# Cross-attention with an FP4 feed-forward on one core: gate and up of a chunk as one alternating run of 24 matmuls

## The reference

```python
def fp4_linear(x, w):
    xq = fp4_quant_dequant(x)
    wq = fp4_quant_dequant(w)
    return jnp.einsum('bsk,nk->bsn', xq, wq)
gate = fp4_linear(x, w_gate)          # 512 -> 1408
y = fp4_linear(x, w_up)               # 512 -> 1408
h = jax.nn.silu(gate) * y
return fp4_linear(h, w_down)          # 1408 -> 512
...
x = x + _L0_ffn_ref(_layernorm(x, axis=-1), L0_ffn_w_gate, L0_ffn_w_up, L0_ffn_w_down)
```

## Time and profile before

| what | value |
|---|---|
| median of 3 runs | 1179.66 us (1179.59 to 1182.97) |
| span of the profiled execution, first to last instruction | 1176.7 us |
| TensorE busy | 1158.8 us, 98% |
| VectorE busy | 970.3 us, 82% |
| ScalarE busy | 483.5 us, 41% |
| GpSimd busy | 179.3 us, 15% |
| feed-forward, tile 2 on | from 467 us to the end |

### The profile page before, as it was taken

How to read it: one execution, slowest core, us unless ns; L and a number is a source line. 1 busy time by engine, 2 the same in 40 slices (tenths; PEclk the granted TensorE clock), 3 DMA queues, 4 the chain that set the end, 5 groups by cost and what they waited for, 6 DMA issues and landing times.

```text
span 1176.7 us, 21716 instructions
## 1 busy us (share of the span) xinstructions
PE 1158.8 (98%) x6784; PEld 1057.6 (90%) x6784; DVE 970.3 (82%) x1609; ACT 483.5 (41%) x1201; POOL 179.3 (15%) x305
## 2 busy tenths in 40 slices
PE   7899999999999999999999999999999999999998
PEld 6688888888888889999999999999999999999997
DVE  6778888888888877988888888888888888888865
ACT  3556656566566553333332332233233323333321
POOL 3433333333333310000000000000000000000000
PEclk9999999999999999999999999999999999999999
DMA  7223323323344436554445345444534454453442
GB/s 240 45 89 88 111 88 110 91 84 111 108 139 148 132 108 194 150 105 86 89 89 102 70 93 99 88 88 87 105 70 93 98 90 88 82 104 76 82 85 46
DMA packets 154955, 119.30 MB, mean 101 GB/s; under 512 B 95597, under 2 KB 122301, under 8 KB 154660
## 3 DMA queue, kind: packets, MB, share of 16 engines
q1 hardware_dynamic: 154916, 118.85, 42.7%
HBM read 74.47 MB, written 24.94 MB: 84 GB/s over the span
## 4 chain that ended last, share of the span: by engine, by line
PE 78%; SPq 7%; DMA 7%; DVE 2%; ACT 2%; issue 2%; POOL 2%; POOLq 0%; DVEq 0%; ACTq 0%
PE g_ps L175 7%; PE u_ps L175 7%; PE u_ps L176 7%; PE g_ps L176 7%; PE u_ps L177 7%; PE g_ps L177 7%; PE d_ps L1436 6%; PE d_ps L1437 6%; PE d_ps L1435 6%; SPq L504 4%; DMA ws_dram<-w_rows 4%; PE o_ps L784 3%; PE s_ps L764 3%; DMA w_wide<-ws_dram 3%; POOL w_q L586 2%
## 5 line engine op out<-in xcount | busy, mean ns | idle before, releaser
L175 PE MATMUL g_ps<-wguh,xnh 128*128 128x352 f32 x496 | 162.4, 327 | 0.5 <-issue 0.5
L175 PE MATMUL u_ps<-wguh,xnh 128*128 128x352 f32 x496 | 159.9, 322 | 0.5 <-DVE hid L1576 0.5
L176 PE MATMUL u_ps<-wgul,xnh 128*128 128x352 f32 x496 | 159.8, 322 | 0.0
L176 PE MATMUL g_ps<-wgul,xnh 128*128 128x352 f32 x496 | 159.8, 322 | 0.0
L177 PE MATMUL u_ps<-wguh,xnl 128*128 128x352 f32 x496 | 159.6, 322 | 0.0
L177 PE MATMUL g_ps<-wguh,xnl 128*128 128x352 f32 x496 | 159.5, 322 | 0.0
L898 ACT ACTIVATE probs<-s_ps,nsmax 128x77 f32<-128x77 f32 x512 | 113.7, 374 | 92.2 <-DVE nsmax L990 92.2
L1576 DVE TENSOR_TENSOR hid<-u_ps,silu 128x352 f32<-128x352 f32 x128 | 66.8, 522 | 78.1 <-PE u_ps L177 75.8
L1437 PE MATMUL d_ps<-wd,hql 128*128 128x512 f32 x330 | 128.9, 391 | 0.0
L1436 PE MATMUL d_ps<-wd,hqh 128*128 128x512 f32 x330 | 128.9, 391 | 0.0
L1435 PE MATMUL d_ps<-wd,hqh 128*128 128x512 f32 x330 | 128.4, 389 | 0.0
(11 more groups left out here) (175 smaller groups left out, 2547.1 us busy)
## 6 DMA issues: line engine op xcount, KB each, us to landing
scale_wide<-st_dram SPq DMA_DIRECT2D x248, 88.0 KB, 3.4
xin<-in_x_dram SPq DMA_DIRECT2D x32, 256.0 KB, 2.8
x_dram<-x SPq DMA_DIRECT2D x32, 256.0 KB, 2.2
xin<-x_dram SPq DMA_DIRECT2D x32, 256.0 KB, 2.7
out_dram<-y SPq DMA_DIRECT2D x32, 256.0 KB, 2.1
scale_wide<-st_dram SPq DMA_DIRECT2D x248, 32.0 KB, 1.8
w_wide<-ws_dram SPq DMA_DIRECT2D x240, 32.0 KB, 1.9
wd_dram<-wd_out SPq DMA_DIRECT2D x11, 512.0 KB, 3.0
```

The costliest lines, as they stand in the source:

```text
L175: pe.matmul(out, lh, rh, start=(i == 0), stop=False)
L176: pe.matmul(out, lh, rl, start=False, stop=False)
```

## The change

Gate and up of one chunk become one run. `pair_matmuls` issues, for each of the 4 blocks, six matmuls that alternate between the gate bank and the up bank: both high by high, both high by low, both low by high. Both waits stand at the head of the run. `gate_done` is raised by the last matmul but one, `up_done` by the last. Up of (0,1), whose gate the attention's code has issued, keeps its own 12 matmuls. In iteration 2 the transposition of the scales stands behind the run of chunk 1. The code of the other engines stays.

```diff
+def pair_matmuls(pe, gate_out, up_out, steps):
+
+    n = len(steps)
+    for i, (xh, xl, gh, gl, uh, ul) in enumerate(steps):
+        pe.matmul(gate_out, xh, gh, start=(i == 0), stop=False)
+        pe.matmul(up_out, xh, uh, start=(i == 0), stop=False)
+        pe.matmul(gate_out, xh, gl, start=False, stop=False)
+        pe.matmul(up_out, xh, ul, start=False, stop=False)
+        gate_last = pe.matmul(gate_out, xl, gh, start=False, stop=(i == n - 1))
+        up_last = pe.matmul(up_out, xl, uh, start=False, stop=(i == n - 1))
+    return gate_last, up_last
...
-            def gate(t, c):
+            def gate_up(t, c):
...
                 if reached(GU * t + c - 1):
                     pe.wait_ge(silu_ready, GU * t + c - 1)
-                split_matmuls(pe, g_ps[:, c % 2, 0:GU_N], [
...
-            def up(t, c):
...
                     pe.wait_ge(hid_ready, GU * t + c - 1)
-                split_matmuls(pe, u_ps[:, c % 2, 0:GU_N], [
+                gated, upped = pair_matmuls(pe, g_ps[:, c % 2, 0:GU_N], u_ps[:, c % 2, 0:GU_N], [
+                    (high[:, d, :], low[:, d, :], k.wguh[:, d, gcols], k.wgul[:, d, gcols],
+                     k.wguh[:, d, ucols], k.wgul[:, d, ucols]) for d in range(EC)
+                ])
+                gated.then_inc(gate_done, 1)
+                upped.then_inc(up_done, 1)
...
                 if valid(a):
                     if reached(a):
-                        gate(a, 1)
+                        gate_up(a, 1)
+                    else:
+                        second_up()
                     if third:
                         scales_transposed(a - 1)
-                    up(a, 1)
                     if not reached(a):
                         f.transpose(pe, 1)
-                    gate(a, 2)
-                    up(a, 2)
-                    gate(a, 3)
-                    up(a, 3)
+                    gate_up(a, 2)
+                    gate_up(a, 3)
```

More of the change, by code:

```diff
@@ L1379, in gate, with second_up @@
                 high, low = halves_of(t)
-                cols = slice(c * GU_N, (c + 1) * GU_N)
+                gcols = slice(c * GU_N, (c + 1) * GU_N)
+                ucols = slice(FF + c * GU_N, FF + (c + 1) * GU_N)
                 if reached(GU * t + c - 1):
                     pe.wait_ge(silu_ready, GU * t + c - 1)
-                split_matmuls(pe, g_ps[:, c % 2, 0:GU_N], [
-                    (high[:, d, :], low[:, d, :], k.wguh[:, d, cols], k.wgul[:, d, cols]) for d in range(EC)
-                ]).then_inc(gate_done, 1)
-            def up(t, c):
-                high, low = halves_of(t)
-                cols = slice(FF + c * GU_N, FF + (c + 1) * GU_N)
-                if reached(GU * t + c - 1):
-                    pe.wait_ge(hid_ready, GU * t + c - 1)
-                split_matmuls(pe, u_ps[:, c % 2, 0:GU_N], [
+                    pe.wait_ge(hid_ready, GU * t + c - 1)
+                gated, upped = pair_matmuls(pe, g_ps[:, c % 2, 0:GU_N], u_ps[:, c % 2, 0:GU_N], [
[4 more added lines that the diff above has]
+                upped.then_inc(up_done, 1)
+            def second_up():
+                high, low = halves_of(0)
+                cols = slice(FF + GU_N, FF + 2 * GU_N)
+                split_matmuls(pe, u_ps[:, 1, 0:GU_N], [
                     (high[:, d, :], low[:, d, :], k.wguh[:, d, cols], k.wgul[:, d, cols]) for d in range(EC)
@@ L1442, in iteration @@
                 if valid(a) and reached(a):
-                    gate(a, 0)
-                    up(a, 0)
+                    gate_up(a, 0)
                 third = isinstance(a, int) and a == 2
```

## The result

| | before | after |
|---|---|---|
| median of the runs | 1181.14 us (4 runs) | 1190.1 us (1188.22 to 1191.66, 4 runs) |
| ratio, 95% interval | | 1.0076 (1.0061 to 1.0091) |
| span of the profiled execution | 1176.7 us | 1189.9 us |
| first gate matmul to last instruction | 748.9 us | 757.6 us |
| start of (2,0), (2,2), (2,3) after the first gate matmul | 39.58, 47.41, 51.94 us | 41.50, 53.87, 60.31 us |

The kernel became 0.76% slower, about 9 us. The median lies 0.1 us above the forecast's range. Before was run once more beside the changed kernel, at 1182.63 us, which moved its own median up by 1.5 us.

What follows compares the result with a forecast made beforehand. The prediction took TensorE's back-to-back matmul stream to bound the feed-forward. Start-up gaps of 5.6 us, 0.3 at the end and 1.4 for the clock sum to 7.3 us on 1179.66, giving 1187.0 us, range 1183.0 to 1190.0.

Steps and rivals of the forecast that it cites:

- What bounds the kernel: Feed-forward: TensorE runs matmuls back to back, busy 596.61 of 596.61 us in the loop, so any new gap is lost time.
- Alternation costs 0: Gate and up matmuls: changing the output bank at every matmul costs 0, with rhythms worth 2.2 us either way.
- Silu 0.27 us later: Each chunk's end: the product also waits for gate's silu, so VectorE runs 0.27 us later; the end wait grows 0.3 us.
- The wait holds in the loop: Loop: up's wait for the product of chunk c-2 comes 1.92 us earlier but is still met, cost 0.
- First gap 1.76 us: Ahead of (2,0): the later silu of (1,3) delays xnh and xnl, so TensorE stands idle for 1.76 us.
- Second gap and third step: Ahead of (2,2): the later scales delay the product of (2,0), and all 24 matmuls wait, not 12: 1.92 us each.
- Clock: Wait ahead of (2,2): TensorE's granted clock falls in the 4.3 us stand, costing 1.4 us, bounds 0 and 1.7.
- The range: Whole-run time: 1183.0 to 1190.0 us, from the forecast case and the case without a fall of the clock, with their bounds.

Runs made afterwards that it cites:

- old start: The changed kernel with tiles 0 to 2 in the old order (gate, then up, scales turned between the halves of (2,1)): 1179.61 us, ratio 1.0002.
- late silu: The kernel before, with gate's end told to ScalarE only by up's last matmul but one: 1181.28 us, ratio 1.0017.
- scales early: The changed kernel with the scales of tile 1 turned behind chunk (2,0) instead of behind (2,1): 1181.7 us, ratio 1.0024.
- wait only: The kernel before, with the wait for the product of chunk c-2 moved from the head of up to that of gate: 1183.62 us, ratio 1.0033.
- filled gap: The changed kernel with 18 matmuls whose result is never read put into the gap ahead of (2,2): 1186.2 us, ratio 1.0053.
- both mended: The changed kernel with chunk (1,3) in the old order and the scales of tile 1 turned behind (2,0): 1179.44 us, ratio 0.9993.
- before with the scales early: The kernel before, old order, with the scales of tile 1 turned behind chunk (2,0): 1178.19 us, ratio 0.9982.

## Why the prediction was right or wrong

Sign and mechanism were right, the size was short: 7.3 us forecast, 8.7 us between the two profiles' feed-forwards and 9.0 us between the medians. The term that failed is the clock's.

- *What bounds the kernel*: right. The stream of matmuls has no slack, and in the feed-forward each us of a new gap came out as a us of time. No loop tile got longer.
- *Alternation costs 0*: right in the loop, by the old start (596.63 us). In the first tiles (1,3) starts 0.1 us later than before (35.74 against 35.64 us after the first gate matmul).
- *Silu 0.27 us later*: right. In the loop the product of (13,1) now starts 0.37 us after up's last matmul has ended (0.11 before), and the wait at the end went from 0.2 to 0.5 us. The late silu alone reproduces it. The Trainium skill (Perfetto Trace Analysis, Optimizing Tensor Performance, Matmuls) says that groups should rotate through banks so that the evacuation of one overlaps the matmuls of the next. The trace agrees as far as this goes: up's 12 matmuls no longer cover gate's silu, hence the 0.37 us; in the loop, though, that costs TensorE nothing.
- *The wait holds in the loop*: right, no wait of TensorE in tiles 4 to 29.
- *First gap 1.76 us*: right. The late silu alone moves (2,0) by 1.76 us; in the changed kernel it is 1.9, with the 0.1 us that was there by (1,3). The releaser was xnl, as forecast.
- *Second gap and third step*: (2,2) was forecast at 481.40 - 427.79 = 53.61 us after the first gate matmul and started at 53.87. The scales early took the chain away, the wait only gave the 1.9 us of the half alone.
- *Clock*: the step that failed, by its size. The fall was forecast, at 1.4 us with a bound of 1.7 from the setup's gap; it cost 2.6 us (6.44 - 3.84, and the same 2.6 by the filled gap). The setup's gap was taken as the bound, but its 1.70 us lost are all that the windows of the earlier trace rows hold (1.00 stands again from 15 us on), while here the clock stood at 0.50 for the whole of the 5.4 us of matmuls from 486.10 to 491.50, and 5.4 x 0.5 = 2.7 us are lost there alone, by this estimate. With 1.60 x 0.41 = 0.7 us in the gap that is 3.4 us withheld against 1.70: the lowered stretch was about twice as long as the setup's, and most of it lay behind the gap. One fall's price is no upper bound for another's. That the clock would fall at all was argued from the length of one gap, and that argument was thinner than it looked: in the changed kernel's own setup a gap of 2.36 us left the clock at 1.00 (last section). The Trainium skill (TensorE: Matmul & The Clock Gate, What's actually happening) says that the throttled clock is the resting state and that activity releases it. The trace agrees with the direction in the gap ahead of (2,2), 1.00 to 0.50 and back behind 5.4 us of matmuls; the size had to be measured.
- *The range*: with 2.6 for 1.4 the sum is 8.5 us, and 0.1 of the 0.2 us that are left was there by (1,3). The range ended at 1190.0 and the median is 1190.1, with before's own median 1.5 us higher than the one I started from. The noise of the runs (3.4 us among four runs of either kernel) had no place in the range, and the upper bound of the clock was too low.

## What to carry to other kernels

A run that is merged from two groups tells of the first group's end late and holds the second group's wait early; in this loop, where the product of (13,1) is done 2.7 us before TensorE asks for it, both were free, and in the first tiles, where no other work stands ahead, both were paid in full. So look at the start of a pipeline by itself, chain by chain, and put what other engines wait for (here one transposition of scales) ahead of the merged run. A gap in a dense stream of matmuls costs its length and, where the clock falls in it, the slow matmuls behind it too; here useless matmuls in a gap that stayed open saved 2.6 us.

## What the runs showed of the hardware that was not expected

- The price of a fall of the clock differs: 1.6 us behind a gap of 2.45 us and 1.7 in the setup behind 2.52, 2.6 and 2.8 us behind gaps of 4.38 us. In the feed-forward it did not fall behind gaps of 1.13 to 1.68 us. That the longer lowered stretch goes with the longer gap was seen in two falls against two; what decides its length was not tried.
- The length of a gap alone does not decide whether the clock falls. Ahead of the same transposes of the setup it held behind 2.36 us in the changed kernel and fell behind 1.92 us in the late silu (a row of TensorE and a window, first of the changed kernel, then of the late silu):

```profile
11.72 3.70 PE L663 MATMUL tp<-ident,w_nat 128*128 128x128 f32 x16 [2.36 <-DMA w_nat<-in_L_xattn_Wq_dram]
12.00:14.00 2.00, 2.00 (x11) 2.00 (x11) 0.50 (x1) 0.88 (x2) 0.00 (x0) 1.00 1.04 381
...
11.46 3.49 PE L652 MATMUL tp<-ident,w_nat 128*128 128x128 f32 x16 [1.92 <-DMA w_nat<-in_L_xattn_Wq_dram]
12.00:14.00 2.00, 2.00 (x11) 1.83 (x10) 0.81 (x2) 1.19 (x2) 0.00 (x0) 0.50 1.01 358
```

  In both mended it fell in the last steps of the attention, around a gap of 1.32 us; the nine other profiles have that gap too, 1.32 to 1.36 us, and keep 1.00 there. So the 1.68 us without a fall are an observation of these traces and no bound. What else decides was not tried.
- The same stream of matmuls runs in several rhythms. In the loop of most runs chunk c = 2 takes 158.3 ns a step and c = 3 160; c = 1, behind the transposition, takes 161.0 from its second matmul on, and the down projection's 33 matmuls 7.52 us. In the scales early and both mended, with the same loop code as the changed kernel, c = 1 takes 160.3 ns and the down projection 7.50 us. With smaller shares of the rest that is 0.04 us per tile, the 1.0 us by which their loops are shorter; the expectations of the last two runs put all of it down to c = 1, which has less than half. In before with the scales early the faster rhythm was there for tiles 4 to 6 alone (68.70 us from the first to the second row below, where before has 68.84) and gone from tile 7 on:

```profile
513.19 0.32 PE L175 MATMUL g_ps<-wguh,xnh 128*128 128x352 f32 x1
...
581.89 0.32 PE L175 MATMUL g_ps<-wguh,xnh 128*128 128x352 f32 x1
```

  It came only in the three runs whose scales are turned behind (2,0), with the alternating order and with the old one; what sets it and what ends it stay open.
